# Sums of probabilities in the later batches: one wide VectorE add a unit instead of adds shared with GpSimd

## The reference, cut to what matters

```python
q = _qdq(layernorm(x)) @ _qdq(wq).T + bq
k, v = split(ctx @ wkv.T + bkv, 2)
attn = softmax(einsum('bnhd,bmhd->bhnm', q, k) * scale)
o = einsum('bhnm,bmhd->bnhd', attn, v).reshape(B, N, C)
x = x + tanh(g_xattn) * (_qdq(o) @ _qdq(wp).T + bp)
x = x + tanh(g_ffn) * ffn(layernorm(x))   # down(silu(gate(x)) * up(x))
```

## Time and profile before

| | us |
|---|---|
| median of 3 runs (lowest to highest) | 1011.36 (1009.93 to 1013.87) |
| the profiled execution | 1011.8, span 1010.0 |
| busy in the span: PE, DVE, ACT, POOL | 885.5, 728.5, 554.4, 397.2 |
| attention stage of batches 1, 2, 3 | 344.6 to 440.9, 579.3 to 675.9, 814.3 to 906.7 |
| exponentials (line 815) | 256 of 1.02 |
| adds on DVE (line 1061), on POOL (line 671) | 114, 207.8 in all; 48, 141.3 |

### The profile page before, as it was taken

The page is one execution under the profiler, slowest core; times in us unless marked ns, Lnnn a source line. Parts: engine busy times, 40 slices in busy tenths (PEclk is TensorE's granted clock), DMA queues, the critical chain, the costliest instruction groups (busy, mean ns, idle before and its releaser), DMA issues.

```text
span 1010.0 us, 13421 instructions
## 1 busy us (share of the span) xinstructions
PE 885.5 (88%) x4872; PEld 312.4 (31%) x4880; DVE 728.5 (72%) x1274; ACT 554.4 (55%) x693; POOL 397.2 (39%) x284
## 2 busy tenths in 40 slices
PE   5978888998999988879999988879899998874898
PEld 2421211144333311135333311125333321122443
DVE  6888969657677779977667779978666778766322
ACT  4547776643565576733566476752556567651230
POOL 1145888720176164540057154470012144470130
PEclk9998999999999998889999988889999998876799
DMA  9234344300211432000211331000200132100001
GB/s 323 76 95 122 102 110 125 104 1 18 51 32 48 123 82 48 1 1 2 50 39 44 106 98 44 21 1 1 47 1 1 37 103 51 37 1 0 1 1 42
DMA packets 37106, 55.27 MB, mean 55 GB/s; under 512 B 8944, under 2 KB 15152, under 8 KB 37040
## 3 DMA queue, kind: packets, MB, share of 16 engines
q1 hardware_dynamic: 35120, 48.13, 16.7%
q0 software_dynamic: 1920, 6.29, 2.2%
HBM read 31.21 MB, written 4.19 MB: 35 GB/s over the span
## 4 chain that ended last, share of the span: by engine, by line
PE 55%; DVE 23%; ACT 10%; issue 8%; POOL 3%; DMA 1%; DVEq 0%; ACTq 0%; POOLq 0%
PE ps L1294 31%; DVE acc L1061 13%; PE ps L1623 8%; ACT r L815 5%; PE ps L1415 4%; PE ps L1436 4%; PE ps L1453 3%; POOL acc L671 2%; PE ps L1477 2%; PE ps L1278 1%; DVE am L917 1%; PE ps L1467 1%; DVE r L1037 1%; ACT r L843 1%; DVE r L1193 1%
## 5 line engine op out<-in xcount | busy, mean ns | idle before, releaser
L815 ACT ACTIVATE r<-ps 128x1024 f32<-128x1024 f32 x256 | 251.6, 1023 | 114.6 <-PE ps L1436 77.7
L671 POOL TENSOR_TENSOR acc<-r,acc 128x1024 f32<-128x1024 f32 x48 | 141.3, 2943 | 177.2 <-ACT r L815 172.6
L1061 DVE TENSOR_TENSOR acc<-acc,r 128x1024 f32<-128x1024 f32 x90 | 179.5, 2016 | 17.9 <-POOL acc L671 9.6
L1436 PE MATMUL ps<-qst,kst 97*128 97x512 f16 x512 | 150.8, 407 | 26.4 <-ACT r L815 25.0
L1453 PE MATMUL ps<-r,vv 128*32 128x512 f32 x1024 | 146.7, 647 | 19.0 <-ACT r L815 14.4
L1037 DVE CUSTOM_DVE_ANT_0 kst<-ps,kst 128x512 f32<-128x512 f32 x192 | 124.5, 686 | 34.5 <-PE ps L1415 32.9
L773 ACT ACTIVATE kst<-ps 128x1024 f32<-128x1024 f32 x96 | 98.2, 1022 | 56.4 <-PE ps L1350 56.1
L689 POOL TENSOR_TENSOR r<-xq,r 128x512 f16<-128x512 f32 x48 | 57.3, 1193 | 145.8 <-ACT r L868 145.4
L1294 PE MATMUL ps<-xs,w_gate 128*128 128x512 f16 x384 | 92.6, 385 | 1.5 <-DVE xs L1225 1.5
L1436 PEld LDWEIGHTS ps<-qst,kst 97*128 97x128 f16 x512 | 37.8, 100 | 181.2 <-ACT r L815 128.9
L1294 PE MATMUL ps<-xs,w_up 128*128 128x512 f16 x384 | 91.2, 380 | 0.0
(11 more groups left out here) (149 smaller groups left out, 1308.2 us busy)
## 6 DMA issues: line engine op xcount, KB each, us to landing
kst<-k_reg SPq DMA_DIRECT2D x192, 64.0 KB
qst<-q_reg SPq DMA_DIRECT2D x192, 32.0 KB
xs<-in_x SPq DMA_DIRECT2D x4, 1024.0 KB, 5.9
cf<-in_ctxT POOLq DMA_DIRECT2D x16, 256.0 KB, 3.4
xres<-in_x SPq DMA_DIRECT2D x4, 1024.0 KB, 5.3
out<-xres SPq DMA_DIRECT2D x16, 256.0 KB, 2.0
acc<-in_down_w SPq DMA_DIRECT2D x10, 256.0 KB, 2.6
vv<-in_wkvT SPq DMA_DIRECT2D x2, 1024.0 KB, 9.9
```

The costliest lines, as they stand in the source:

```text
L671: nc.gpsimd.tensor_tensor(sums, prob[:, p:p + 2, :], sums, ALU.add).then_inc(p_pool, 1)
L815: nc.scalar.activation(prob[:, s:s + 2, :], ps[:, first_bank:first_bank + 2, :], ACT.Exp, scale=SCALE).then_inc(exp_done, 1)
L1061: nc.vector.tensor_tensor(sums, other, prob[:, p:p + 2, :], ALU.add).then_inc(p_dve, 1)
L1436: mm = nc.tensor.matmul(bank(first_bank + k), kst[0:97, g % 2, j + k, t * P:(t + 1) * P], qst[0:97, g % 2, j + k, :], start=True, stop=True)
```

## The change

In batches 1 to 3 the adds leave POOL. Per batch 26 of the 32 units are added, all by DVE, all four heads in one 128x2048 operation; the first of a group again joins units 0 and 1, so there are 22 operations. The six others (tile 7 of each group and tile 3 of groups 1 and 2) go through `sums` on PE as in batch 0. The bank of totals is therefore started by unit 7's `sums`. The totals of a group run at t == 0 of the next group, not at t == 1. ACT waits, for both exponentials of a unit, for the one add that frees the slot of three units before. The oT copy waits for the values alone (o_full). On POOL the inverse deviation of the next x and the bias of xres now come first in the stage.

```diff
-ADDS = {}
...
+ADDED = ((0, 1, 2, 3, 4, 5, 6), (0, 1, 2, 4, 5, 6), (0, 1, 2, 4, 5, 6), (0, 1, 2, 3, 4, 5, 6))
+ADD_HEADS = HG
+ADD_PARTS = HG // ADD_HEADS
+ADD_UNITS = [g * MT + t for g in range(G) for t in ADDED[g][1:]]
...
-            def add_units(b):
...
-                    nc.gpsimd.tensor_tensor(sums, prob[:, p:p + 2, :], sums, ALU.add).then_inc(p_pool, 1)
-                    if n == 1 and b < B - 1:
-                        inverse_deviation(variance_of_x(b + 1))
-                residual_bias(b)
...
-                    add_units(b)
+                    if b < B - 1:
+                        inverse_deviation(variance_of_x(b + 1))
+                    residual_bias(b)
...
-                            index = ADD_OF[freed, j // 2]
-                            act.wait_ge({"POOL": p_pool, "DVE": p_dve}[index[0]], add_count(b, index))
+                            act.wait_ge(p_dve, add_count(b, freed, j + 1))
...
-                        if added(b, u - 1):
-                            act.wait_ge(p_used, b * UNITS + u)
-                        else:
-                            act.wait_ge(o_full, g)
+                        act.wait_ge(o_full, b * G + g)
...
+                for j in range(0, HG, ADD_HEADS):
+                    sums, p = acc[:, j:j + ADD_HEADS, :], p_slot(b, u, j)
+                    dve.wait_ge(exp_done, pair_count(b, u, j + ADD_HEADS - 1))
+                    if first:
+                        q = p_slot(b, u - 1, j)
+                        other = prob[:, q:q + ADD_HEADS, :]
+                    else:
                         other = sums
...
+                        dve.wait_ge(p_dve, add_count(b, ADD_UNITS[ADD_UNITS.index(u) - 1], j))
+                    nc.vector.tensor_tensor(sums, other, prob[:, p:p + ADD_HEADS, :], ALU.add).then_inc(p_dve, 1)
...
-                                          prob[:, p_slot(b, u, j), :], start=(u == 0), stop=(u == UNITS - 1))
+                                          prob[:, p_slot(b, u, j), :], start=(u == (MT - 1 if b else 0)), stop=(u == UNITS - 1))
...
-                                          start=(g == 0), stop=False)
+                                          start=False, stop=False)
...
-                    if b > 0 and t == 1 and g > 0:
+                    if b > 0 and t == 0 and g > 0:
                         totals(b, g - 1)
```

More of the change, by code:

```diff
@@ L239, in added, with add_count @@
 def added(b, u):
[L240 to L246, removed]
+    return b > 0 and u % MT in ADDED[u // MT]
+def add_count(b, u, j):
+    at = u + 1 if u % MT == 0 else u
+    return ((b - 1) * len(ADD_UNITS) + ADD_UNITS.index(at)) * ADD_PARTS + j // ADD_HEADS + 1
 def p_slot(b, u, j):
@@ L412, in build @@
         s_full, exp_done, p_used = sem("s_full"), sem("exp_done"), sem("p_used")
-        p_pool, p_dve, acc_read = sem("p_pool"), sem("p_dve"), sem("acc_read")
+        p_dve, acc_read = sem("p_dve"), sem("acc_read")
         o_full, o_out, den_out = sem("o_full"), sem("o_out"), sem("den_out")
@@ L1040, in maxima, with add_unit @@
                     ins.then_inc(m_free, 1)
[L1042 to L1051, removed]
-                        other = sums
[L1053 to L1061, removed]
+            def add_unit(b, u):
+                if u not in ADD_UNITS:
+                    return
+                g = u // MT
+                first = u % MT == ADDED[g][1]
+                if first and g > 0:
+                    dve.wait_ge(acc_read, (b - 1) * (G - 1) + g)
+                elif first:
+                    dve.wait_ge(x_done, b * NT)
+                    dve.wait_ge(ctx_ready, min(b + 1, B - 1) * CHUNKS)
+                for j in range(0, HG, ADD_HEADS):
[5 more added lines that the diff above has]
+                    else:
+                        other = sums
+                        dve.wait_ge(p_dve, add_count(b, ADD_UNITS[ADD_UNITS.index(u) - 1], j))
+                    nc.vector.tensor_tensor(sums, other, prob[:, p:p + ADD_HEADS, :], ALU.add).then_inc(p_dve, 1)
             dve.wait_ge(split_hi, CT)
@@ L1168, in _ @@
                     else:
-                        add_units(b, u)
+                        add_unit(b, u)
                     for _ in range(W_UNITS[u] if b == 0 else 0):
@@ L1467, in sums @@
                     mm = nc.tensor.matmul(ps[j * DH:(j + 1) * DH, DEN_BANK, :], esel[:, g, :],
-                                          prob[:, p_slot(b, u, j), :], start=(u == 0), stop=(u == UNITS - 1))
+                                          prob[:, p_slot(b, u, j), :], start=(u == (MT - 1 if b else 0)), stop=(u == UNITS - 1))
                 mm.then_inc(p_used, 1)
             def totals(b, g):
-                for h in range(2):
-                    index = ADD_INDEX[g, h, len(ADDS[g, h]) - 1]
-                    pe.wait_ge({"POOL": p_pool, "DVE": p_dve}[index[0]], add_count(b, index))
+                pe.wait_ge(p_dve, add_count(b, g * MT + ADDED[g][-1], HG - 1))
                 for j in range(HG):
                     mm = nc.tensor.matmul(ps[j * DH:(j + 1) * DH, DEN_BANK, :], esel[:, g, :], acc[:, j, :],
-                                          start=(g == 0), stop=False)
+                                          start=False, stop=False)
                 if g < G - 1:
```

## The result

The changed kernel takes 955.64 us, median of four (953.65 to 955.89), against 1011.54 before: a ratio of 0.944, interval 0.942 to 0.946. Forecast were 963.6 and a range of 949 to 982. The profiled execution took 953.65 with a span of 951.8.

The account below looks back on a forecast made before the run. Bound: PE's chain, with DVE's adds late because of POOL's adds beside them. Stages of 79.6, 79.6 and 78.1, together 237.3 against 285.3 us, gain 48.0: 1011.8 - 48.0 = 963.8, given as 963.6, range 949 to 982.

Parts of the forecast that it names:

- (b): DVE's adds: 38 a batch become 22 of 128x2048, each 2.28 us, 2.37 a link, 52 us a batch against 69.3.
- first group: Start of each stage: ACT's waits for DVE's adds 1 to 6, 5.3 us in batches 1 and 2, 3.8 in batch 3.
- slot waits, groups 1 to 3: ACT waiting for adds to free slots: 0.45 x 3 plus 1.07 for add 9 beside the bias, 2.4 us a stage.
- sums and totals together, two: PE at units 16 and 24: two extra blocks before the next scores, 1.1 us lost each, 2.2 a stage.
- What the stage could do: ACT's pace where nothing waits, read in batch 3: 0.98 us an exponential, 1.96 a unit; PE's two blocks just fit in.
- (f): POOL's bias of xres, now first, runs beside adds 4 to 10: 1.07 us each for adds 5, 6 and 9.
- (e): ACT's slots freed by whole units, units 8g and 8g+1 together by one add: 0.4 to 0.45 us lost a group.
- The rest is untouched: Outside the three stages: batch 0 and what follows denT keep their times, so no gain there.
- Rival 1: More is gained: PE's extra blocks fit in ACT's shadow, add 6 is in time, stages about 74, 949 us; chance 0.13.
- Rival 2: Dearer handover: adds at 2.44 or PE at its lower clock level behind waits, 975 to 985 us; chance 0.18 over 974.
- Rival 3: Slower: DVE bounds the stage if a wide add takes 3.7 us or more; at 6.4, 1200 us; chance 0.03.
- Rival 4: No gain: waits on whole units eat DVE's saving, stages still 92 or more, 1000 to 1012 us; chance 0.04.

Follow-up runs that it names:

- e1: The changed kernel with 16 idle POOL adds of 128x1024 put back into each later attention stage; 1040.72 us, ratio 1.029 to the kernel before.
- e3: The kernel before with only the six units a stage moved to sums on PE, other adds narrow and shared with POOL; 979.75 us, ratio 0.969.
- g1: The changed kernel with all units but unit 31 added on DVE, run once more for a trace of its stages; 997.39 us, one execution.
- e2: The changed kernel with each wide add split into two of 128x1024 on DVE; 952.66 us, ratio 0.943 to the kernel before.
- g3: f3 with group 2's extra PE unit dropped in batches 1 and 2, and only unit 31 on PE in batch 3; 943.98 us, ratio 0.934.
- f1: The changed kernel with POOL's bias of xres waiting for group 1's last add; 955.01 us, ratio 0.944 to the kernel before.
- f2: The changed kernel with 31 of 32 units added on DVE, 27 wide adds a stage, only unit 31 on PE; 998.24 us, ratio 0.986.
- g2: The kernel before with POOL's adds given to DVE, none to PE: 31 units in halves, totals in the second unit, bias after group 1; 962.41 us, ratio 0.953.
- f3: The changed kernel with adds in halves, totals in the next group's second unit and bias after group 1; 941.66 us, ratio 0.931 to the kernel before.
- e4: The changed kernel with the totals moved back to the second unit of the next group; 950.37 us, ratio 0.940 to the kernel before.

## Why the prediction was right, and where it was off

The direction, the mechanism (DVE's adds free of POOL's company, e1) and the place were right. The profiled execution took 953.65 us where the sum had 963.8: 5.7 of the 10.2 us lie in the stages (231.6 against 237.3), 4.5 outside them. In batch 3's stage terms that are 1.9 us too high and terms that are 1.1 too low leave 0.9, so that its fit is in part luck. Term by term, for batch 3's stage and, where it differs, batch 1's:

| term | predicted | measured |
|---|---|---|
| wide add (b) | 2.28 | 2.29, with its wait 2.40 |
| exponentials and oT copies | 64.2 | 63.1; 63.0 |
| first group | 3.8; 5.3 | 4.1; 3.8 |
| slot waits, groups 1 to 3 | 2.4 | 1.6 |
| sums and totals together, two | 2.2 | 2.5; 2.7 |
| sums alone, two | 1.4 | 1.6 |
| tail | 4.1 | 4.4 |
| stage | 78.1; 79.6 | 77.2; 77.1 |

- **What the stage could do.** I read 0.98 us an exponential as ACT's pace. It was PE's: the first six take 5.66 us, so (5.66 - 1.02) / 5 = 0.93 each, and four behind a wait take 3.77, (3.77 - 1.02) / 3 = 0.92 each. PE's two blocks, 0.97 + 0.99, were the bound I called "just fit in". This is the term of 1 us too much, and it is why ACT makes up part of a wait on DVE while a block on PE costs 0.8 to 0.9 in full.
- **First group, batches 1 and 2**, the largest miss, 1.5 us. A statistics step and an add take 2.80 us together, 350.26 to 353.05 in DVE's timeline, not 0.70 + 2.37: the wait for the own result passes beside the step in between. Unit 7 and 8 wait 0.77 each in place of 1.1, unit 9 1.67 in place of 2.6.
- **The bias (f).** 1.07 on add 9 and, in batches 1 and 2, on add 6 was wrong. In batch 1 the bias runs from 361.70 to 370.47, beside the end of add 6 and all of add 9, and both keep their 2.29 us; the POOL operation that met add 9 took 3.33. What it lengthened there are the scaling steps of x, which I had at 0.48 and which take 1.50 beside it:

```profile
361.70 8.77 POOL L630 TENSOR_TENSOR xres<-xres,bp_bc 128x512 f32<-128x512 f32 x4
...
367.04 2.29 DVE L1041 TENSOR_TENSOR acc<-r 128x2048 f32<-128x2048 f32 x1 [0.99 <-ACT r L797]
369.25 1.50 DVE L930 TENSOR_SCALAR xs<-xs,mv,rstd 128x512 f32<-128x512 f32 x1
```

  In batch 3 adds 5 and 6 were lengthened, to 3.18 and 3.19 us (0.9 each in place of 1.07), and the wait of 2.57 was as forecast (2.7); with the bias gone it is 1.64.
- **The rest is untouched.** The four other stretches gave 4.5 us, which I had at zero. 1.1 lie before batch 1, in code that is the same, and the start of that stage also varies between 343.5 and 344.8 in these kernels. 3.2 lie behind batch 3's denT, where PE ran at its upper level for blocks that had run at the lower. Before, and after:

```profile
908.25 3.49 PE L1278 MATMUL ps<-identf,k_reg 128*128 128x128 f32 x16
...
942.07 3.57 PE L1294 MATMUL ps<-xs,w_gate 128*128 128x512 f16 x8 [1.49 <-DVE xs L1225]
```

```profile
852.83 1.96 PE L1258 MATMUL ps<-identf,k_reg 128*128 128x128 f32 x16
...
885.63 1.89 PE L1274 MATMUL ps<-xs,w_gate 128*128 128x512 f16 x8 [1.49 <-DVE xs L1205]
```

  The transposes follow a PE that had waited 3.88 us for DVE before and 1.25 after; but e3 and e1 have them at full speed behind waits of 4.54 and 3.67, so that the wait is not the whole cause, and it stays open. The second block is slow in the traces of three kernels, before, e1 and e3, whose last exponential and denT lie 8.7 us and more apart in batch 3, and fast in the traces of ten others, where they are 4.4 or less apart: this part goes with the change's shorter tail. The three other executions of the changed kernel took 1.9 to 2.2 us longer than this one.
- **Rival 1** (blocks in ACT's shadow) did not occur; each block shows in full as a wait of ACT. **Rival 2** did not: the link came to 2.40 us, not 2.44 with more on top, and the clock stayed at 1.00 in the stages behind waits of up to 1.96 us. How near that part of the rival was, the length of the wait does not tell: the clock fell behind 3.2 to 6.1 us in g1 and e2, but also behind 1.85 in g3 and 1.25 in f1's batch 2. **Rival 3** has e1 as its nearest case: with 16 POOL adds a stage beside them, the same wide adds give 1040 us. I had priced it at two whole narrow adds beside POOL, 6.4 us, where a wide add loses only one POOL operation: 4.39. **Rival 4** did not occur; stages as long as its own were seen in g1 (90 to 93 us), but there from late totals behind five more adds, not from the slot waits of (e).
- **What I gave no term of its own** is how much the six units on PE matter. I counted them as a cost of 0.7 to 1.1 us each. Without five of them the changed kernel takes 998 us (f2) in place of 956, and with the old place, halves and late bias 962 (g2) against 942 (f3), two kernels that differ in these units alone. So they carry the totals' new place, and give DVE the time to keep pace.

## What to carry to other kernels

An engine that helps another can cost more than it does: compare the helped operation's time with and without company (3.22 against 1.22 us here) before splitting work. When a chain in order waits for a side result, try moving the waiting instruction behind the work that others need next (e4, 4 to 5 us), and take some pieces out of the side work (g2 to f3, 21 us). Then take single edits together: three that gave 9 us one by one gave 14 together, because the cost of one was the wait that another removes. When a steady pace is read, look at how fast the engine goes just behind a wait: if it is faster there (0.92 against 0.98 us), the pace belongs to somebody else.
